# An LSTM with a residual: VectorE takes over the residual add and the low part of x; GpSimd keeps only the maximum over partitions

## The reference

```
xW = x @ Wx + b                       # Wx: 512 x 2048
for t in range(512):
    a = xW[:, t] + h @ Wh             # Wh: 512 x 2048, h: 32 x 512
    i, f, o = sigmoid(a[:, 0:512]), sigmoid(a[:, 512:1024]), sigmoid(a[:, 1024:1536])
    g = tanh(a[:, 1536:2048])
    c = f * c + i * g
    h = o * tanh(c)
    out[:, t] = x[:, t] + h
```

## Time and profile before

| | us |
|---|---|
| median of 3 runs | 2901.87 (2901.34 to 2902.7) |
| the profiled execution, its own time | 2904.1 |
| its span, first to last instruction | 2902.2 |
| PE busy, share of the span | 2738.0, 94% |
| DVE busy | 1967.8, 68% |
| ACT busy | 1238.9, 43% |
| POOL busy | 630.4, 22% |
| mean granted TensorE clock | 0.99 |
| HBM traffic over the span | 38 GB/s |

### The profile page before, as it was taken

One profiled execution on the slowest core, in us unless ns is written; L12 is line 12 of the kernel. 1 busy time (PEld: TensorE's weight loads), 2 busy tenths in 40 slices (PEclk: granted clock), 3 DMA queues, 4 the chain that ended last, 5 costly groups with the idle time before them and its releaser, 6 DMA issues.

```text
span 2902.2 us, 122776 instructions
## 1 busy us (share of the span) xinstructions
PE 2738.0 (94%) x49152; PEld 1276.7 (44%) x49152; DVE 1967.8 (68%) x7481; ACT 1238.9 (43%) x3722; POOL 630.4 (22%) x902
## 2 busy tenths in 40 slices
PE   3999999999999999999999999999999999999998
PEld 0444444444444444444444444444444444444444
DVE  6666666666666666666666666666666666666666
ACT  2444444444444444444444444444444444444444
POOL 0222222222222222222222222222222222222221
PEclk6999999999999999999999999999999999999999
DMA  6111111111111111111111111111111111111110
GB/s 135 35 40 33 33 40 36 33 33 41 35 33 36 40 33 33 43 33 33 37 39 33 33 39 37 33 33 41 35 33 36 40 33 33 41 35 33 36 41 24
DMA packets 223520, 109.94 MB, mean 38 GB/s; under 512 B 25216, under 2 KB 222464, under 8 KB 222464
## 3 DMA queue, kind: packets, MB, share of 16 engines
q1 hardware_dynamic: 223488, 109.48, 15.2%
HBM read 75.83 MB, written 33.55 MB: 38 GB/s over the span
## 4 chain that ended last, share of the span: by engine, by line
issue 39%; PE 25%; DVE 25%; ACT 6%; POOL 3%; POOLq 1%; DMA 0%; DVEq 0%; SPq 0%; ACTq 0%
PE Z L247 25%; DVE h_hi L464 7%; DVE h_lo L494 4%; DVE h L492 3%; DVE x_T L379 3%; ACT tanh_c L359 3%; ACT act L353 3%; POOL y L547 2%; DVE c L479 2%; DVE fc L475 2%; DVE ig L477 1%; DVE xmax L387 1%; DVE c L486 1%; DVE hT_hi L469 1%; POOL xmax_all L518 1%
## 5 line engine op out<-in xcount | busy, mean ns | idle before, releaser
L247 PE MATMUL Z<-wh_hi,hT_hi 128*32 128x512 f16 x8176 | 796.1, 380 | 55.0 <-DVE hT_hi L469 55.0
L353 ACT ACTIVATE act<-Z,scales 128x192 f32<-128x192 f32 x1022 | 427.1, 418 | 926.4 <-PE Z L247 926.4
L247 PE MATMUL Z<-wx_hi,x_hi 128*32 128x512 f16 x8176 | 795.6, 379 | 17.8 <-POOL x_lo L528 17.8
L247 PE MATMUL Z<-wx_lo,x_hi 128*32 128x512 f16 x8176 | 795.6, 379 | 0.0
L247 PE MATMUL Z<-wx_hi,x_lo 128*32 128x512 f16 x8176 | 795.4, 379 | 0.0
L247 PE MATMUL Z<-wh_lo,hT_hi 128*32 128x512 f16 x8176 | 794.6, 379 | 0.0
L247 PE MATMUL Z<-wh_hi,hT_lo 128*32 128x512 f16 x8176 | 532.2, 380 | 55.4 <-DVE hT_lo L497 51.1
L475 DVE TENSOR_TENSOR fc<-act,c 128x64 f32<-128x64 f32 x512 | 115.6, 226 | 672.3 <-ACT act L353 672.3
L547 POOL TENSOR_TENSOR y<-h,x_res 128x128 f32<-128x128 f32 x512 | 228.1, 452 | 1118.1 <-issue 894.5
L464 DVE SCALAR_TENSOR_TENSOR h_hi<-act,scales,tanh_c 128x64 f16<-128x64 f32 x1024 | 392.3, 383 | 113.0 <-ACT tanh_c L359 86.1
L359 ACT ACTIVATE tanh_c<-c 128x64 f32<-128x64 f32 x1024 | 262.4, 256 | 367.5 <-DVE c L486 345.7
(11 more groups left out here) (51 smaller groups left out, 1683.4 us busy)
## 6 DMA issues: line engine op xcount, KB each, us to landing
x_in<-in_x SPq DMA_DIRECT2D x512, 64.0 KB, 2.1
x_res<-in_x SPq DMA_DIRECT2D x512, 64.0 KB, 2.1
out_y<-y SPq DMA_DIRECT2D x512, 64.0 KB, 1.7
wx_raw<-in_Wx SPq DMA_DIRECT2D x16, 256.0 KB, 8.6
wh_raw<-in_Wh SPq DMA_DIRECT2D x16, 256.0 KB, 18.6
bias_bc<-in_bias SPq DMA_DIRECT2D x4, 64.0 KB, 2.0
h_in<-in_h SPq DMA_DIRECT2D x4, 16.0 KB, 13.4
```

What stands on the lines that cost most here:

```text
L247: return nc.tensor.matmul(bank[L * j:L * j + B, :], lhsT, rhs, start=False, stop=last, skip_group_check=True)
L353: nc.scalar.activation(half_gates(act, a)[:, 0:3], half_gates(Z[s], a)[:, 0:3], ACT.Sigmoid, scale=scale).then_inc(sig_done, 1)
```

## The change

POOL loses the scaling and subtraction that make x_lo and the add of x to h; it keeps only `partition_all_reduce`. DVE gets `cut_x_lo`, one `scalar_tensor_tensor` in place of POOL's two operations (so `x_scaled` goes), and `add_x`, at the end of each step, behind the transpose of the low part. `h32` has one buffer. The preparation of the x of the coming blocks stands at new places in DVE's queue: during block n, `turn_x(n+1)` after s=0, `max_of_x(n+2)` after s=1, `cut_x_lo(n+1)` after s=2, `scale_block(n+2)` after s=3; each behind that step's `add_x`. In the preparation DVE makes the scales of block 1 and the low part of block 0 before it cuts the low part of Wh. POOL's `block` is one `partition_all_reduce`. ACT, PE and SP keep their code.

```diff
--- before.py
+++ after.py
@@ -56,7 +56,6 @@
         x_T = sb("x_T", [P, NCH, TB, B])
         x_hi = sb("x_hi", [P, 2, NCH, TB * B], F16)
         x_lo = sb("x_lo", [P, 2, NCH, TB * B], F16)
-        x_scaled = sb("x_scaled", [P, NCH * TB * B])
         x_res = sb("x_res", [P, 2, TB, C])
         y = sb("y", [P, 2, TB, C])
 
@@ -67,7 +66,7 @@
         ig = sb("ig", [P, C])
         c = sb("c", [P, C])
         tanh_c = sb("tanh_c", [P, C])
-        h32 = sb("h32", [P, 2, C])
+        h32 = sb("h32", [P, C])
         h_hi = sb("h_hi", [P, C], F16)
         h_lo = sb("h_lo", [P, C], F16)
         hT_hi = sb("hT_hi", [P, NCH, B], F16)
@@ -124,9 +123,7 @@
         zs_done = sem("zs_done")
         scales_done = sem("scales_done")
         x_turned = sem("x_turned")
-        x_scaled_done = sem("x_scaled_done")
         xmax_seen = sem("xmax_seen")
-        scales_seen = sem("scales_seen")
         x_hi_cut = sem("x_hi_cut")
         x_lo_cut = sem("x_lo_cut")
         xpart_done = sem("xpart_done")
@@ -379,6 +376,18 @@
                 nc.vector.transpose(x_T[:, :, :, :].rearrange("p ch t b -> p t ch b"),
                                     x_in[:, r].rearrange("p t (ch l) -> p t ch l", ch=NCH)).then_inc(x_turned, 1)
 
+            def cut_x_lo(n, r):
+                v.wait_ge(x_hi_cut, n + 1)
+                nc.vector.scalar_tensor_tensor(x_lo[:, r], x_T[:, :, :, :].rearrange("p ch t b -> p ch (t b)"),
+                                               x_scale(r), x_hi[:, r], ALU.mult, ALU.subtract).then_inc(x_lo_cut, 1)
+
+            def add_x(n, i, s, r):
+                if s == 0:
+                    v.wait_ge(res_loaded[r], (i + 1) * (16 * NJ))
+                    if started(i):
+                        v.wait_ge(y_stored[r], i * (16 * NJ))
+                nc.vector.tensor_tensor(y[:, r, s], h32[:, :], x_res[:, r, s], ALU.add).then_inc(y_done, 1)
+
             def max_of_x(n, r, count):
                 v.wait_ge(x_loaded[r], 16 * NJ * count)
                 if started(n):
@@ -456,6 +465,8 @@
                 scale_tables()
                 scale_block(0, 0)
                 max_of_x(1, 1, 1)
+                scale_block(1, 1)
+                cut_x_lo(0, 0)
                 for ch in range(NCH):
                     cut_w_lo(1, ch)
 
@@ -487,11 +498,11 @@
                 turn_high_part(t, 0)
                 high_part_of_h(t, 1, q)
                 turn_high_part(t, 1)
-                if started(t - 1):
-                    v.wait_ge(y_done, t - 1)
-                nc.vector.tensor_tensor(h32[:, s % 2], act[:, 2 * C:3 * C], tanh_c[:, :], ALU.mult).then_inc(h32_done, 1)
+                if started(t):
+                    v.wait_ge(y_done, t)
+                nc.vector.tensor_tensor(h32[:, :], act[:, 2 * C:3 * C], tanh_c[:, :], ALU.mult).then_inc(h32_done, 1)
                 v.wait_ge(h32_done, t + 1)
-                nc.vector.scalar_tensor_tensor(h_lo[:, :], h32[:, s % 2], h_scale(q), h_hi[:, :],
+                nc.vector.scalar_tensor_tensor(h_lo[:, :], h32[:, :], h_scale(q), h_hi[:, :],
                                                ALU.mult, ALU.subtract).then_inc(h_lo_done, 1)
                 v.wait_ge(h_lo_done, t + 1)
                 nc.vector.transpose(hT_lo[:, :, :], h_lo[:, :].rearrange("p (ch l) -> p ch l", ch=NCH)).then_inc(hT_lo_done, 1)
@@ -499,12 +510,16 @@
             def block(i, n, r, has):
                 for s in range(TB):
                     step(n * TB + s, s, r)
+                    add_x(n, i, s, r)
+                    if has(1) and s == 2:
+                        cut_x_lo(n + 1, 1 - r)
                     if has(1) and s == 0:
-                        scale_block(n + 1, 1 - r)
-                    if has(1) and s == 1:
                         turn_x(n + 1, 1 - r, i + 1 + r)
-                    if has(2) and s == 2:
+                    if has(2) and s == 1:
                         max_of_x(n + 2, r, i + 2)
+                    if has(2) and s == 3:
+
+                        scale_block(n + 2, r)
 
             prepare()
             v.wait_ge(c_cleared, 1)
@@ -517,38 +532,16 @@
                 pool.sem_inc(xmax_seen, 1)
                 nc.gpsimd.partition_all_reduce(xmax_all[:, :], xmax[:, :], P, bass.bass_isa.ReduceOp.max).then_inc(xmax_shared, 1)
 
-            def cut_x_lo(n, r):
-                pool.wait_ge(x_turned, n + 1)
-                pool.wait_ge(scales_done, n + 1)
-                pool.sem_inc(scales_seen, 1)
-                nc.gpsimd.tensor_scalar(x_scaled[:, :], x_T[:, :, :, :].rearrange("p ch t b -> p (ch t b)"),
-                                        x_scale(r), None, ALU.mult).then_inc(x_scaled_done, 1)
-                pool.wait_ge(x_scaled_done, n + 1)
-                pool.wait_ge(x_hi_cut, n + 1)
-                nc.gpsimd.tensor_tensor(x_lo[:, r], x_scaled[:, :].rearrange("p (ch tb) -> p ch tb", ch=NCH),
-                                        x_hi[:, r], ALU.subtract).then_inc(x_lo_cut, 1)
-
             for k in range(2):
                 pool.wait_ge(wmax_done, k + 1)
                 nc.gpsimd.partition_all_reduce(wmax_all[:, k:k + 1], wmax[:, k:k + 1], P,
                                                bass.bass_isa.ReduceOp.max).then_inc(wmax_shared, 1)
             share_xmax(0)
-            cut_x_lo(0, 0)
             share_xmax(1)
 
             def block(i, n, r, has):
-                for s in range(TB):
-                    t = n * TB + s
-                    pool.wait_ge(h32_done, t + 1)
-                    if s == 0:
-                        pool.wait_ge(res_loaded[r], (i + 1) * (16 * NJ))
-                        if started(i):
-                            pool.wait_ge(y_stored[r], i * (16 * NJ))
-                    nc.gpsimd.tensor_tensor(y[:, r, s], h32[:, s % 2], x_res[:, r, s], ALU.add).then_inc(y_done, 1)
-                    if has(1) and s == 1:
-                        cut_x_lo(n + 1, 1 - r)
-                    if has(2) and s == 2:
-                        share_xmax(n + 2)
+                if has(2):
+                    share_xmax(n + 2)
 
             run_blocks(pool, block)
```

## The result

| us | before | changed |
|---|---|---|
| median (runs) | 2902.28 (4) | 2725.84 (4: 2725.62 to 2726.29) |
| ratio, 95% interval | | 0.939 (0.9374 to 0.9406) |
| profiled execution, span | 2902.2 | 2724.5 |
| execution's own time | 2904.1 | 2726.29 |
| PE, DVE, POOL busy | 94%, 68%, 22% | 98%, 71%, 2% |

Predicted: 2724, of 2717 to 2748. On the chips of the later runs the kernel before took 2908 to 2932; the changed one took 2725.6 to 2727.2 on the two chips where it was measured. Why the kernel before differs from chip to chip isn't shown; within its one trace the step after s=1 takes 5.18 to 7.02, and in the changed kernel every step takes 5.18.

A forecast was written before the change was run, and what follows sets the result against it. PE, 94% busy, was taken as the bound, with POOL's work lengthening two steps a block. Start 74.75, 510 x 5.18 = 2641.8, old tail 7.05 and 0.35 gave span 2723.95, median 2723.7, told as 2724; range 2717 to 2748.

The forecast's parts named there:

- The floor: Steps of the loop: a short step is bound by PE alone at 5.18, so 510 steps take 2641.8.
- GpSimd's work goes, 179.8 less: Long steps of each block: removing POOL's adds and cuts wins all of the 1.41 a block, 179.8 over 510 steps.
- a late add and a stretched h_hi: Two long steps a block, 5.95 and 5.87: DVE waits for POOL's old add; h_hi takes 1.05 beside POOL's x_lo.
- `add_x`, `turn_x`, `max_of_x`, `scale_block` at nothing: DVE's idle 1.95 a step: the add takes 0.25, with a maximum or scales at most 1.26; all hidden.
- `cut_x_lo` at nothing: DVE after s=2: the cut takes 0.747, is ready by 1504.60, no cost; bounds 0 to 36 us.
- the limit is 1504.74: Latest time for x_lo before PE's x matmuls at 1504.85, leaving at least 0.14.
- the first rival: PE's input part after s=3: x_lo comes 0.25 late in each block, 32 us, so 2756; chance 0.08.
- The wait for the maximum at nothing: `scale_block` on DVE behind POOL's maximum: asked for two steps (10.36) earlier, 1.7 left even with a code change; no cost.
- The preparation +1.2, up to +1.7: Before the loop: step 0 comes 0.60 later, PE gains 0.5 but loses 1.7 at the lower clock; net +1.2, between -0.5 and +1.7.
- The tail +0.35: End of the run: the last add stands behind h_lo and hT_lo, 1.23 against about 0.80; +0.35 taken.
- The rule against the row: DVE's fc beside POOL's maximum lost only 0.05, against the skill's exclusive port lock; by that rule the maximum could still block DVE.
- From span to median: Whole run: own time 1.9 above the span, median 2.2 below that, so span 2723.95 gives median 2723.7.

## Why the prediction was right

- *The floor.* "A short step is bound by PE alone": 510 x 5.18 = 2641.8 predicted, 2641.80 measured. This term carries the result.
- *GpSimd's work goes, 179.8 less.* 2821.60 - 2641.80 = 179.8. The cause is shown in this order: without the change of code 81 go, without the elementwise work the other 97. The reading of a late add and a stretched h_hi was right for what is seen in the block. What moving one alone would do was expected wrongly, 2822 and 2793 where the runs gave 2908 (by the place of the cut) and 3568. The prediction didn't need it, since the change removes both.
- *`add_x`, `turn_x`, `max_of_x`, `scale_block` at nothing*: right, 0.25, 0.70, 0.67 and four small operations in a stretch that keeps 0.96 idle or more.
- *`cut_x_lo` at nothing*: right, 0.741 against 0.747. But "the limit is 1504.74", 0.11 ahead of the matmuls, was read from hT_lo, and doesn't hold for x_lo, which needs 0.23. By the prediction's latest time, 1504.60, and the true limit, 1504.62, the margin was 0.02 and not 0.14. The cut began 0.41 after hT_lo (1513.54 to 1513.95) where 0.59 was allowed, and that alone made it 0.21. So "no cost" came true on a limit that was wrong: that part is luck, and the first rival was nearer than its 0.08.
- *The wait for the maximum at nothing*: right, the maximum is done 9.1 early.
- *The preparation +1.2, up to +1.7*: 75.32 - 73.55 = 1.77. VectorE's step 0 came 0.65 later for 0.60 (68.72), and PE began 0.35 earlier for 0.5 (70.38). The twelve groups of the recurrent part took 4.71, to the next x group at 75.09, against 2.59 at 5.18 a step: 2.1 lost where 1.7 was taken, as some ten of twelve and not nine ran at the lower level, and a group there starts 0.43 and not 0.40 after the one before.
- *The tail +0.35*: 2724.5 - 2717.12 = 7.38 for 7.40.
- *The rule against the row.* The fc of the earlier trace rows began 0.01 before the maximum, so it isn't an operation that found the ports taken, and the row decides nothing. Nor does the changed kernel: its maximum (1509.65 to 1510.00) lies where VectorE is idle.
- *From span to median*: the sum gave a span of 2723.95, measured 2724.5; the median lay 1.3 above the span, where -0.3 was taken (own time 1.9 above, median 2.2 below). That offset makes 1.6 of the 2.1 between 2723.7 and 2725.84, the preparation less the tail the rest.

## What to carry to other kernels

Where an engine is near its floor in most steps, take the floor from an undisturbed step and count what disturbs the others; here that gave the time to 0.1%. An engine that changes between two kinds of work pays for it behind the waits of the first operation of the new kind, so what matters is which operation that is: taking work off it can move the payment onto the path and cost more than the work did. Where a block is a closed loop over two engines, write down its parts before and after: an operation put ahead of the one that starts the loop costs nearly its whole length (0.62 of 0.71 here), and can eat what another part gained.

## What the runs showed of the hardware

- GpSimd between elementwise work and `partition_all_reduce`: 6.1 us from the end of xmax to the start of the maximum, and 6.9 to 7.5 in the blocks shown before elementwise work resumes (6.6 to 7.8 in the kernel before), counted from when the waits ahead of the operation are met. The Trainium skill, GPSIMD Engine Reference, section "Instruction dispatch", has about 6 us for the first call of freshly loaded code; the maximum agrees, the way back is some 1 us more.
- A VectorE operation with two inputs next to a GpSimd one with two inputs waits for its end (h 1.16 for 0.25, ending 0.15 after it); next to one with one input of 128x512 it ends 0.75 after that one's start, which costs 0.22 to 0.24 in the block shown, and at most 0.52 (the longest h of that kernel is 0.773 for 0.249).
- PE reads 512 columns as four runs of 128 as fast as in one (5.18 a step either way).
- TensorE's wait for x_lo, two instructions of its queue ahead of the weight load, costs 0.24 from the end of the VectorE operation; the wait for hT_lo, on the weight load itself, costs 0.06.
